# Unread matmuls in every step of a recurrence that uses TensorE for three tenths of its time

## The reference

```python
def step(carry, xs):
    h, c = carry
    xi_t, xf_t, xg_t, xo_t = xs
    i_t = jax.nn.sigmoid(xi_t + h @ V_i)
    g_t = jnp.tanh(xg_t + h @ V_c)
    o_t = jax.nn.sigmoid(xo_t + h @ V_o)
    c_new = h * c + i_t * g_t
    h_new = o_t * jnp.tanh(c_new)
    return ((h_new, c_new), h_new)
```

## Time and profile before

| what | value |
|---|---|
| median of 3 runs | 2959.77 us (2956.96 to 2959.95) |
| time of the profiled execution | 2956.47 us |
| its span, first to last instruction | 2954.8 us |
| PE busy, matmuls | 1386.3 us (47%) |
| DVE busy | 1920.9 us (65%) |
| ACT busy | 1449.6 us (49%) |
| mean granted TensorE clock | 0.569 |

### The profile page before, as it was taken

One profiled execution on the slowest core, in us unless ns is written; L12 is line 12 of the kernel. 1 busy time (PEld: TensorE's weight loads), 2 busy tenths in 40 slices (PEclk: granted clock), 3 DMA queues, 4 the chain that ended last, 5 costly groups with the idle time before them and its releaser, 6 DMA issues.

```text
span 2954.8 us, 67705 instructions
## 1 busy us (share of the span) xinstructions
PE 1386.3 (47%) x20258; PEld 998.8 (34%) x20258; DVE 1920.9 (65%) x15110; ACT 1449.6 (49%) x8446; POOL 169.7 (6%) x130
## 2 busy tenths in 40 slices
PE   4989867444444444444444444444444444444433
PEld 4434422333333333333333333333333333333322
DVE  6557788666666666666666666666666666666666
ACT  5431123455555555555555555555555555555554
POOL 0530066000000000000000000000000000000000
PEclk8999978555555555555555555555555555555555
DMA  6010000000000000000000000000000000000000
GB/s 251 1 36 1 0 0 6 2 2 2 2 1 2 1 2 2 2 2 2 2 2 2 2 2 2 2 2 2 1 2 2 2 2 2 2 2 2 2 2 16
DMA packets 12829, 26.80 MB, mean 9 GB/s; under 512 B 1971, under 2 KB 9654, under 8 KB 10422
## 3 DMA queue, kind: packets, MB, share of 16 engines
q1 hardware_dynamic: 10406, 22.02, 2.1%
q10 hardware_dynamic: 2064, 0.55, 0.1%
HBM read 21.52 MB, written 1.05 MB: 8 GB/s over the span
## 4 chain that ended last, share of the span: by engine, by line
ACT 43%; PE 30%; DVE 17%; issue 9%; DMA 1%; SPq 0%; POOL 0%; DVEq 0%; POOLq 0%; ACTq 0%
ACT work L667 25%; PE psum L500 15%; DVE work L990 12%; ACT work L658 12%; ACT psum L660 5%; PE psum L504 5%; PE psum L419 4%; PE psum L360 2%; PE psum L371 1%; DVE work L902 1%; DMA work<-in_adj_dram 1%; DVE FT L939 1%; PE psum L399 1%; PE psum L290 1%; DVE X L946 0%
## 5 line engine op out<-in xcount | busy, mean ns | idle before, releaser
L500 PE MATMUL psum<-work,MASK 128*128 128x1 f16 x12288 | 814.9, 169 | 1443.1 <-DVE work L990 1429.0
L500 PEld LDWEIGHTS psum<-work,MASK 128*128 128x128 f16 x12288 | 647.3, 108 | 1630.3 <-DVE work L990 1629.2
L658 ACT ACTIVATE work<-psum 128x1 f32<-128x1 f32 x2048 | 350.7, 171 | 1139.4 <-PE psum L504 1139.4
L667 ACT ACTIVATE work<-psum,work 128x2 f32<-128x2 f32 x2048 | 722.4, 353 | 2.8 <-issue 2.8
L504 PE MATMUL psum<-work,MASK 128*128 128x1 f16 x6144 | 710.7, 172 | 0.0
L987 DVE TENSOR_SCALAR work<-work 128x1 f32<-128x1 f32 x2048 | 315.5, 154 | 527.1 <-ACT work L662 527.1
L504 PEld LDWEIGHTS psum<-work,MASK 128*128 128x128 f16 x6144 | 543.2, 104 | 0.0
L990 DVE TENSOR_TENSOR_SCAN work<-work 128x3 f16<-128x3 f32 x2048 | 341.5, 167 | 279.2 <-ACT work L667 5.9
L1000 DVE SCALAR_TENSOR_TENSOR work<-psum,work 128x1 f32<-128x1 f32 x2048 | 433.4, 212 | 0.0
L1003 DVE TENSOR_TENSOR work<-work 128x1 f32<-128x1 f32 x2048 | 325.8, 159 | 70.5
L662 ACT ACTIVATE work<-psum 128x2 f32<-128x2 f32 x2048 | 354.8, 173 | 0.0
(11 more groups left out here) (142 smaller groups left out, 1061.4 us busy)
## 6 DMA issues: line engine op xcount, KB each, us to landing
work<-in_adj_dram SPq DMA_DIRECT2D x16, 1024.0 KB, 5.0
work<-in_L_ffn_Wd_dram SPq DMA_DIRECT2D x4, 512.0 KB, 6.2
out_dram<-work SPq DMA_DIRECT2D x4, 256.0 KB, 2.4
work<-in_L_ffn_bd_dram SPq DMA_DIRECT2D x1, 512.0 KB, 6.8
W<-in_L_ffn_W_dram ACTq DMA_DIRECT2D x1, 256.0 KB, 2.8
watt<-in_L_gnn_w_att_dram ACTq DMA_DIRECT2D x2, 64.0 KB, 6.9
work<-in_L_gnn_Wq_dram SPq DMA_DIRECT2D x1, 64.0 KB, 9.3
Wfc<-in_L_gnn_W_fc_dram ACTq DMA_DIRECT2D x1, 64.0 KB, 5.5
```

What stands on the lines that cost most here:

```text
L500: nc.tensor.matmul(into, Vparts[:, gate, part, :], h_steps[:, q, 2:3], start=False, stop=False, skip_group_check=True)
L658: nc.scalar.activation(sig_i[:, q], bank(NGATE * k)[:, col:col + 1], ACT.Sigmoid, scale=1.0 / SCALE_V).then_inc(i_ready, 1)
L667: nc.scalar.activation(Z[:, t % 2, 0:3:2], bank(6 + t % 2)[:, 0:1].to_broadcast([P, 2]), ACT.Tanh, bias=hc[:, q], scale=sig_i[:, q]).then_ ...
```

## The change

TensorE gets matmuls whose results nobody reads. `keep_busy` issues a number of them: 128 x 128 weights (the bf16 identity), 448 moving columns from the mask of the first attention, written into columns 64 to 511 of a bank. 28 of them are put ahead of the transposes before the recurrence. In each step three are put behind the nine matmuls of the gates, into the third bank of the set that is not in use; in the three steps of a half block that hold an input matmul there are two. The bias and input matmuls move from steps 2 to 7 of a half block to steps 56 to 61.

```diff
+            def keep_busy(b, times):
+
+                for part in range(times):
+                    nc.tensor.matmul(bank(b)[:, HALF:CH], identity_b[:], MASKT[:, part % NGATE, 0:CH - HALF],
+                                     start=False, stop=False, skip_group_check=True)
+
+            keep_busy(1, 28)
             transpose_rows(3, range(2), b0=6)
...
                     gate_sum(0, i_summed)
                     gate_sum(1, g_summed)
                     gate_sum(2, o_summed)
-                    if t - col + HALF < N and col in (2, 4, 6):
-                        gate_biases(1 - k, col // 2 - 1)
-                    if t - col + HALF < N and col in (3, 5, 7):
-                        gate_inputs(1 - k, col // 2 - 1, t - col + HALF)
+                    keep_busy(NGATE * (1 - k) + 2, NGATE - col % 2 if 56 <= col < 62 else NGATE)
+                    if t - col + HALF < N and col in (56, 58, 60):
+                        gate_biases(1 - k, (col - 56) // 2)
+                    if t - col + HALF < N and col in (57, 59, 61):
+                        gate_inputs(1 - k, (col - 56) // 2, t - col + HALF)
```

## The result

The changed kernel takes 2940.22 us (median of 4 runs, 2934.6 to 2941.21) against 2958.36 us before: a ratio of 0.9939, 95% interval 0.9923 to 0.9955. It is faster, by 0.6% where 2.4% was forecast, and lies 2 us outside the range. The clock did what was forecast and the step did not.

The account below looks back on a forecast made before the run. The prediction took the recurrence's step, a chain of waits repeated 2048 times at half clock, as the bound. From 2956.5 us it took 70 for the faster step and added 1 for bias matmuls: 2888 us, range 2810 to 2938 us.

Parts of the forecast that it names:

- The clock: TensorE's granted clock: with unread matmuls in each step, full clock through the whole recurrence in place of half.
- The unread matmul and its cover: Behind the gates: each streams 0.187 us at full clock; three cost nothing, ending before the next weight load is due.
- Gate i, 0.014 us a step: Gate i's matmuls in the recurrence step, 0.19 us long, gain 0.014 us at full clock; bounds 0.008 and 0.033 us.
- the isolated form: Line 360's longest matmul, after a wait with its own weight load: 1219 and 697 ns; gives gate i 0.008 us.
- the stream: Line 360's shortest matmul, in a stream: 1061 and 592 ns at the two clocks; gives gate i 0.033 us.
- the tail that halves too: Rival: single columns speed up like streamed matmuls and ScalarE follows; step gains 0.05 to 0.073 us, 2807 to 2855 us; chance 0.17.
- Gate g: Gate g's three pairs behind gate i, 0.08 us at half clock: gain 0 to 0.04 us a step, 0.02 taken.
- the rule that was weighed: Skill's rule: TensorE starts never under some 25 ns apart; gate g would gain 3 x 2 ns, sum 2917 us.
- Bias matmuls, at most 1 us: Bias pair behind three unread matmuls: nothing to 0.01 us late in 3 x 31 steps, at most 1 us.
- The 28 ahead as nothing: 28 unread matmuls before the recurrence: delay of nothing to 3.6 us against some 4 us saved, counted as nothing.
- the first rival: Weight load and single-column matmul pairs don't speed up: gain 0.014 us a step, 2929 us (2916 to 2941); chance 0.22.
- the 70: Forecast gain in us over the recurrence: 2048 steps x 0.034 us; bounds 16 and 150 us.

## Why the prediction was wrong

*The clock* was right: full clock in the recurrence but for its first three steps, and a rise by itself where TensorE does not rest.

*The unread matmul and its cover* were right: 187 ns of streaming, and in ordinary steps the next gates wait for VectorE and not for line 477.

*Gate i, 0.014 us a step:* right, slightly mis-sized. Over the whole trace line 665 starts 0.514 us after line 997, where line 658 stood at 0.524 (medians): 0.010 us, most of the 0.012 that the step gained. Line 510 of gate i lasts 178 ns at most where line 504 lasted 187. So the isolated form of the earlier trace rows, which gives 0.008 us, was the right one to lean on and the stream the wrong one; the tail that halves too (2807 to 2855 us) did not occur.

*Gate g is the step that failed:* "Gain 0 to 0.04 us; I take the middle, 0.02 us." The middle stood for want of a row, and the engines at both ends refuse it. On TensorE three pairs fell from 0.080 to 0.075 us: six of them span ScalarE's starts from 1502.50 to 1502.65, where the earlier trace rows has 1500.52 to 1500.60 for three. That is 25 ns a pair, the figure of the rule that was weighed. And on ScalarE even a gain of 25 ns would have been lost, as the runs with gate g earlier show. Over the whole trace line 665 to line 674 is 0.268 us where line 658 to line 667 was 0.270 (medians): gate g brought 0.002 us in place of 0.02. 2048 x 0.02 = 41 us of the 70 rested on it, and some 4 us came.

*Bias matmuls, at most 1 us:* mis-sized. They cost 8.6 us, 0.092 us in each of 93 steps. The unread matmuls end where they were put, but the bias's weight load starts 0.09 us later, and from there to the next step's load it is 0.37 us, not the 0.31 that half of the earlier trace rows's 0.62 gave. These pauses beside one-row weights were not in the sum, and the run with 128 rows removes them. The first could be read in the kernel before, where it costs nothing because TensorE is free then. Pairs stand 0.027 us apart there, but the bias's weight load 0.09 us behind the last line 504:

```profile
1437.99 0.17 PE L504 MATMUL psum<-work,MASK 128*128 128x1 f16 x1
...
1438.08 0.49 PEld L479 LDWEIGHTS psum<-ones,MASK 1*128 1x128 f32 x2
```

*The 28 ahead as nothing:* right to within the 1.7 us above.

So the first rival held, pairs that don't speed up (2916 to 2941 us, given 0.22): its 2929 us and the 8.6 us of the bias matmuls make 2938, and without these, in the run with 128 rows, the kernel stands where that rival put it, at 2928 us. The range, which ended at 2938, left off that rival's upper edge, and the bias matmuls, counted as 1 us, carried the kernel past it.

## What to carry to other kernels

A faster engine shortens a chain only by what the engine alone sets in it: before pricing closer results, read from the next engine whether it can take them closer, and a pitch that always equals its supplier's proves nothing about its own; issuing the second result sooner in a run of its own tells it at once. Work put in to hold the clock belongs to a budget with two edges: enough that the clock stays up even in the steps that hold other work, and not so much that it stands ahead of the next dependent instruction. Here it was best issued without a wait of its own: where the clock fell, in the run with two unread matmuls, it was low for 3.4 to 6.8 us at a time, and for some 100 us with the wait. Where matmuls of few rows stand between full ones, try padding them to the same number of rows; here that gave 8.6 us back.

## What the runs showed of the hardware that was not expected

Weight load and single-column matmul pairs on TensorE came 27 ns apart at half clock and 25 ns at full: doubling the clock gained 2 ns. Two ScalarE instructions behind one another ended no closer together when the second's input came sooner: it started 13 ns sooner (68 against 81 ns behind the first) and lasted 11 ns longer (167 against 156). The weight load of a one-row fp32 matmul started 0.09 us after the streaming of 128-row weights was over, and pairs of either kind in turn 0.36 us apart at full clock, where 128-row pairs alone came 0.23 us apart. And a step whose unread matmuls wait on another engine took 1.167 us at full clock and 1.69 us at half, and stayed at half for some 100 us, until steps came in which TensorE did not wait.
